# Routed experts of a two-layer hybrid block: the down product as one unsplit fp32 matmul a block

## The chip, the cores and the metric

The kernel runs on one core of one Trainium2 chip. The metric is the device time of one execution in microseconds (us); smaller is better. Three runs of the kernel before took 1002.78, 1001.38 and 1005.39 us, median 1002.78.

## The reference, cut to what matters

The model is a chain of a Mamba-1 mixer, a mixture-of-experts layer, a Mamba-2 mixer with a gated MLP, and the same mixture-of-experts layer again, over 2048 tokens of width 128. The change touches only the two mixture-of-experts layers, and of these only the routed experts:

```
x         = tokens, 2048 x 128
prob      = softmax(x @ gate_weight.T)          # 8 experts
top 2 experts of each token, weights normalised
routed(x) = sum over the two experts e of weight * swiglu(x, gate_up[e], down[e])
swiglu(x, gate_up, down):
    h = x @ gate_up.T                           # 128 -> 2 * 938
    g, u = split(h)
    return (silu(g) * u) @ down.T               # 938 -> 128
```

The output adds a shared expert of the same shape, which every token passes, and the residual.

## The kernel before, in words

`ffn_stage` is built twice, with the tags `f` (first layer) and `g` (second); `f_` and `g_` begin the tiles' names in the profile. Tokens are sorted by expert into 39 tiles (`SLOT_TILES`) of 128 token slots. Each expert's slots are padded to whole tiles. A table, filled at run time, tells for each tile its expert and where the expert's weights lie: a ring of three places (`RING`), each holding an expert's gate-up weights (2 x 938 columns) and down weights (8 blocks, `TILES`, of 128 rows, the last with 42 real ones).

Most products of the layer are made in split precision. A number is cut into a high part, rounded to fp32r (the format that TensorE takes in one reduced-precision product), and a low part, which is the rest. Three products of parts (high by high, high by low, low by high) make one accurate product. `raw_ring` and `ring` are the same memory under two types: plain fp32, and rounded fp32r. SyncE loads an expert's raw weights into `raw_ring` (`load_expert`), and GpSimd splits them in four parts in `split_part`: part 0 copies the gate-up weights to their high half (L1047), part 1 the down weights (L1049), part 2 writes the low half of gate-up (L1052), part 3 that of down (L1055) and raises `w_ready`. Which part follows which gather of token rows or which store of result rows on GpSimd's queue is written out by hand (`BEHIND_GATHER`, `BEHIND_STORE`). Expert n+3 is loaded once the last product with expert n is summed.

TensorE's order for tile j (L1247 on) is: transpose the 128 token rows of tile j (`turn_row`, L1229); down product of tile j-2 (`down_tile`, L1214 and L1217); transpose the products silu(g) * u of tile j-1 (`turn_products`, L1196, eight blocks); gate and up products of tile j in two halves of columns (`expert_half`, L1243 to L1245, twelve matmuls). Token tiles and products stand in pairs of buffers by the tile's parity.

In `down_tile` each of the eight blocks takes two matmuls. The first (L1214) has the high part of the turned products (`q_hi`) as its stationary operand, and 256 moving columns: the high and the low half of the down weights side by side. Its results lie in the columns 0 to 127 and 128 to 255 of the PSUM bank `Y2`. The second (L1217) has the low part `q_lo` stationary and the 128 high columns moving; the last block has none. Its 42 real rows have their low part in further rows of the same stationary tile, from row 64 (`UT`) on, against a second copy of the weights there. So there are 15 matmuls a tile. After them ScalarE scales the cross columns by the tokens' share into `cross` (`crossed`, L1400), VectorE adds them to the main columns times the share and writes the result rows (`finish`, L1752), and GpSimd stores the rows (L1078).

The turned products are 1024 columns in two PSUM banks. ScalarE copies both halves to `q_hi` (L1395), VectorE subtracts that from PSUM and writes `q_lo` (L1742), and for the last block's tail one more small subtraction into `q_hi` (L1746). ScalarE's SiLU is L1418, VectorE's product L1773. TensorE waits for these through `q_low`, and before it writes the bank of the next down product, for `outs_ready`.

Of the kernel before, what the change touches and what calls it, by code (L numbers as in the profile page):

```python
# [16 lines left out]
P = 128  # L17
BATCH, SEQ = 2, 1024
T = BATCH * SEQ
CH = 512  # L20
# [23 lines left out]
EW = 2 * GW + 2 * TILES * P  # L44
# [794 lines left out]
def ffn_stage(k, d, which, tag, cleared, ready, out=None, logs=None, following=None):  # L839
# [39 lines left out]
    cross = work[:, 2 * H0:2 * H0 + 2 * P].rearrange("p (b m) -> p b m", b=2)  # L879
# [13 lines left out]
    def gathered(j):  # L893
# [9 lines left out]
        prods_ready, prods_turned, q_high, q_low, cross_ready, outs_ready, both_ready, tokens_ready, out_added, \  # L903
# [5 lines left out]
            "prods_ready prods_turned q_high q_low cross_ready outs_ready both_ready tokens_ready out_added "  # L909
# [14 lines left out]
    LAST_ROWS = UT + 2  # L924
# [51 lines left out]
    def down_of(ring, place):  # L976
        return ring[:, place, 2 * GW:EW].rearrange("p (i h m) -> p i h m", i=TILES, h=2)

    with stage, nc.Block(no_gpsimd_drain=True) as block:  # L979

        @block.sync
        def _(sp):
            def load_expert(n):
                place = (n - 1) % RING
                low, dn, done = raw_ring[:, place, GW:2 * GW], down_of(raw_ring, place), w_loaded[place]
                sp.dma_start(low[:, 0:INTER], d["gu"][n - 1, :, 0:INTER]).then_inc(done, 16)
                sp.dma_start(low[:, INTER:GW], d["gu"][n - 1, :, INTER:GW]).then_inc(done, 16)
                sp.dma_start(dn[:, :, 1, :], d["dn"][n, :, :].rearrange("(i p) m -> p i m", p=P)).then_inc(done, 16)
# [44 lines left out]
        def _(pool):  # L1033
            PARTS, STORES = 4, 2
            GROUPS = [0] + list(range(4, SLOT_TILES, 2))
            BEHIND_GATHER = {3: [(2, 0), (2, 1), (2, 2), (2, 3)], 5: [(3, 0)], 7: [(3, 1)], 9: [(3, 2)], 11: [(3, 3)],
                             17: [(4, 0)], 19: [(4, 1)], 21: [(4, 2)], 23: [(4, 3)],
                             33: [(5, 0), (5, 1), (5, 2), (5, 3)], 35: [(6, 0), (6, 1)], 37: [(6, 2)], 38: [(6, 3)]}
            BEHIND_STORE = {1: [(7, 0)], 3: [(7, 1), (7, 2), (7, 3)], 7: [(8, 0)], 9: [(8, 1)], 11: [(8, 2)], 13: [(8, 3)]}

            def split_part(n, part):
                place = (n - 1) % RING
                high, low, dn = ring[:, place, 0:GW], ring[:, place, GW:2 * GW], down_of(ring, place)
                raw, raw_dn = raw_ring[:, place, GW:2 * GW], down_of(raw_ring, place)
# [53 lines left out]
        def _(pe):  # L1098
# [31 lines left out]
            def gate_up(q):  # L1130
# [15 lines left out]
                if q == NPRE + 2:  # L1146
                    pe.wait_ge(q_low, 2 * SLOT_TILES)
# [58 lines left out]

            def down_tile(j):
# [141 lines left out]
        def _(act):  # L1349
# [57 lines left out]
            def tile(j):  # L1407
                if j:
                    turned(j)
                if j >= 2:  # L1410
                    crossed(j - 2)
# [53 lines left out]
            crossed(SLOT_TILES - 2)  # L1465
            evac(SLOT_TILES - 1)
            silu(NPRE)
            crossed(SLOT_TILES - 1)
# [35 lines left out]
        def _(dve):  # L1504
# [232 lines left out]
            def evac(j):  # L1737
                for half in range(2):
                    dve.wait_ge(q_high, 2 * j + half + 1)
                    n = CH - half * P  # L1740
                    a = slice(half * CH, half * CH + n)
                    last = nc.vector.tensor_tensor(q_lo[:, j % 2, a], ps[:, TR + half, 0:n],  # L1742
                                                   q_hi[:, j % 2, a].bitcast(F32), ALU.subtract)
                    if half:
# [1007 lines left out]
```

## Time and profile before

| What | Value |
|---|---|
| median of 3 runs | 1002.78 us |
| the profiled execution's own time | 1002.86 us |
| its span | 1001.0 us |
| TensorE matmul busy | 953.4 us (95%), 4711 records |
| TensorE weight load busy | 676.2 us (68%) |
| VectorE busy | 725.1 us (72%) |
| ScalarE busy | 569.8 us (57%) |
| GpSimd busy | 616.6 us (62%) |
| DMA | 69.71 MB, 70 GB/s on the mean |

In the rows, PE is TensorE's matmul, PEld its weight load, which overlaps matmuls, PEldq the sequencer that feeds them, DVE VectorE, ACT ScalarE, POOL GpSimd. A record's duration runs from its start to its modelled end, so durations of pipelined matmuls overlap; what one costs in a dense stream is the distance from its start to the start of the next. A plain fp32 matmul shows as two records of PE and two of PEld, a transpose or an fp32r matmul as one of each.

### The profile page before, as it was taken

To read this page: it belongs to the slowest core of one execution; us is meant where nothing else is said; L and a number is where in the kernel's file an instruction comes from. 1 tells how busy PE (TensorE), PEld (TensorE's weight loads), DVE (VectorE), ACT (ScalarE), POOL (GpSimd) and SP (SyncE) were. 2 spreads that over 40 slices of the span, in tenths; PEclk is the share of its full clock that TensorE was granted. 3 is DMA by queue.
4 is the path that set the end of the run, shared out by engine and by line. 5 is a ranking of instruction groups with operands and counts; after the bars stand their busy time and mean duration, and the time that the engine had idled before them with its cause. 6 is when DMAs were issued, how large, how long until landed. Compare 5 with 4: busy or idle time off the path is not lost. (4 is left out here: it accounts for less than half of the span.)

```text
span 1001.0 us, 16162 instructions
## 1 busy us (share of the span) xinstructions
PE 953.4 (95%) x4711; PEld 676.2 (68%) x4711; DVE 725.1 (72%) x1192; ACT 569.8 (57%) x1046; POOL 616.6 (62%) x482
## 2 busy tenths in 40 slices
PE   7988999988999999999999999998999999999997
PEld 2323333332467799899998556666666999999996
DVE  3999998999588666566665797775597666566666
ACT  6764655655542555555554788787723555555553
POOL 1599897999531856686541397852305764967432
PEclk9999989998999999999999999999999999999999
DMA  5233223353341123232011300000702222421104
GB/s 158 67 77 80 77 82 71 90 118 86 112 123 55 33 84 89 75 82 81 28 33 42 112 1 1 2 1 1 225 0 71 79 68 64 123 74 31 33 24 132
DMA packets 69248, 69.71 MB, mean 70 GB/s; under 512 B 14952, under 2 KB 51568, under 8 KB 69168
## 3 DMA queue, kind: packets, MB, share of 16 engines
q1 hardware_dynamic: 64176, 58.44, 20.2%
q0 software_dynamic: 4992, 10.23, 3.7%
q8 instruction: 46, 0.75, 0.3%
q14 instruction: 34, 0.28, 0.1%
HBM read 58.00 MB, written 10.62 MB: 69 GB/s over the span
## 5 line engine op out<-in xcount | busy, mean ns | idle before, releaser
L810 POOL TENSOR_TENSOR a_hc<-a_h,a_c_sb 128x512 f32<-128x512 f32 x128 | 159.7, 1272 | 45.1 <-DVE a_h L711 45.0
L492 PE MATMUL ps<-a_hc,eye 128*128 128x512 f32 x256 | 134.5, 641 | 12.6 <-POOL a_hc L810 12.0
L629 ACT ACTIVATE ps<-a_delta,a_neg_a 128x512 f32<-128x512 f32 x128 | 87.1, 689 | 73.5 <-DVE a_h L711 70.6
L492 PEld LDWEIGHTS ps<-a_hc,eye 128*128 128x128 f32 x256 | 45.6, 195 | 80.3 <-POOL a_hc L810 43.8
L1067 POOL DMA_INDIRECT f_rows<-xn_rows,f_source x39 | 37.4, 958 | 70.1 <-DVE f_source L1700 35.5
L1067 POOL DMA_INDIRECT g_rows<-xn_rows,g_source x39 | 37.3, 956 | 69.1 <-DVE g_source L1700 38.1
L711 DVE TENSOR_TENSOR_SCAN a_h<-ps,a_state,a_b_u 128x512 f32<-128x512 f32 x64 | 79.0, 1278 | 1.0 <-ACT ps L629 0.8
L1214 PE MATMUL ps<-g_ring_rounded,g_q_hi_rounded 128*128 x312 | 77.1, 337 | 0.0
L1214 PE MATMUL ps<-f_ring_rounded,f_q_hi_rounded 128*128 x312 | 77.0, 337 | 0.0
L711 DVE TENSOR_TENSOR_SCAN a_h<-ps,a_b_u 128x512 f32<-128x512 f32 x64 | 75.2, 1212 | 1.9 <-ACT ps L629 1.7
L691 DVE TENSOR_TENSOR a_b_u<-a_du,ps 128x1024 f32<-128x1024 f32 x57 | 68.5, 1202 | 0.9 <-PE ps L479 0.8
L1078 POOL DMA_INDIRECT token_rows<-f_rows,f_back x39 | 38.0, 975 | 49.0 <-DMA token_rows<-f_rows,f_back 23.3
L1078 POOL DMA_INDIRECT token_rows<-g_rows,g_back x39 | 38.0, 975 | 44.2 <-DMA token_rows<-g_rows,g_back 19.2
L1243 PE MATMUL ps<-f_ring_rounded,f_work_rounded 128*128 x156 | 62.1, 398 | 3.0 <-POOL f_ring_rounded L1055 1.8
L1773 DVE TENSOR_TENSOR f_prods<-f_work,ps 128x470 f32<-128x470 f32 x78 | 50.3, 644 | 18.0 <-PE ps L1245 14.3
L1243 PE MATMUL ps<-g_ring_rounded,g_work_rounded 128*128 x156 | 62.0, 397 | 1.0 <-DVE g_work_rounded L1758 0.6
L1418 ACT ACTIVATE f_work<-ps 128x470 f32<-128x470 f32 x78 | 44.0, 565 | 32.8 <-PE ps L1245 30.7
L1418 ACT ACTIVATE g_work<-ps 128x470 f32<-128x470 f32 x78 | 44.0, 564 | 30.2 <-PE ps L1245 27.4
L1773 DVE TENSOR_TENSOR g_prods<-g_work,ps 128x470 f32<-128x470 f32 x78 | 50.3, 644 | 14.9 <-PE ps L1245 11.1
L1217 PE MATMUL ps<-f_ring_rounded,f_q_lo_rounded 128*128 x273 | 60.9, 223 | 0.0
L1217 PE MATMUL ps<-g_ring_rounded,g_q_lo_rounded 128*128 x273 | 60.9, 223 | 0.0
L1214 PEld LDWEIGHTS ps<-g_ring_rounded,g_q_hi_rounded 128*128 128x128 f32 x312 | 58.9, 189 | 2.8
(485 smaller groups left out, 2753.3 us busy)
## 6 DMA issues: line engine op xcount, KB each, us to landing
a_c_sb<-c_rows SPq DMA_DIRECT2D x64, 256.0 KB, 3.3
f_ring<-in_gu SPq DMA_DIRECT2D x16, 469.0 KB
g_ring<-in_gu SPq DMA_DIRECT2D x16, 469.0 KB
f_ring<-in_dn SPq DMA_DIRECT2D x8, 512.0 KB
g_ring<-in_dn SPq DMA_DIRECT2D x8, 512.0 KB
xn_rows<-f_work SPq DMA_DIRECT2D x8, 256.0 KB, 4.1
f_rows<-token_rows SPq DMA_DIRECT2D x8, 256.0 KB, 4.7
xn_rows<-g_work SPq DMA_DIRECT2D x8, 256.0 KB, 4.1
```

The lines of the kernel that those rows point to most:

```text
L492: nc.tensor.matmul(ps[:, Y + f, :], k.eye[:, :], hc[:, s % WAITING, :], start=False, stop=(n == NST - 1)).then_inc(y_added, 1)
L629: nc.scalar.activation(ps[:, A + m % NA, :], delta[:, f, cols(g)], ACT.Exp, scale=neg_a[:, f, n:n + 1])\
L691: nc.vector.tensor_tensor(decayed_in[:, p:p + FT, :], du[:, :, cols(g)], ps[:, B + i % 2, :].unsqueeze(1).to_broadcast([P, FT, CH]), ALU.m ...
L711: nc.vector.tensor_tensor_scan(h[:, s % DEPTH, :], ps[:, A + m % NA, :], decayed_in[:, m % FEED, :], initial, ALU.mult, ALU.add).then_inc( ...
L810: nc.gpsimd.tensor_tensor(hc[:, m % WAITING, :], h[:, s % DEPTH, :], c_sb[:, i % RING, :], ALU.mult)\
L1067: nc.gpsimd.indirect_dma_start(rows[:, j, :], None, k.xn_rows, bass.IndirectOffsetOnAxis(ap=source[:, j:j + 1], axis=0))\
L1078: nc.gpsimd.indirect_dma_start(k.token_rows, bass.IndirectOffsetOnAxis(ap=back[:, j:j + 1], axis=0), rows[:, j, :], None).then_inc(sent, 16)
L1214: last = nc.tensor.matmul(ps[:, Y2, 0:2 * P], q_hi[:, j % 2, a], in_ring(place, w, w + 2 * P), start=(i == 0), stop=(i == NI), skip_group_ ...
L1217: nc.tensor.matmul(ps[:, Y2, 0:P], q_lo[:, j % 2, a], in_ring(place, w, w + P), start=False, stop=False, skip_group_check=True)
L1243: nc.tensor.matmul(out, xt[:, 0, j % 2, :], w_hi, start=True, stop=False)
L1418: nc.scalar.activation(gates[:, half, 0:HALVES[half]], ps[:, 2 * half, 0:HALVES[half]], ACT.Silu)\
L1773: nc.vector.tensor_tensor(prods[:, j % 2, half * H0:half * H0 + HALVES[half]], gates[:, half, 0:HALVES[half]], ps[:, 2 * half + 1, 0:HALVE ...
```

## The change

The down product of the routed experts is made in plain fp32. The turned products go unsplit into `q_plain`, an fp32 view of the memory that `q_hi` is in; the first half is copied by ScalarE, the second by VectorE. The down weights stay as SyncE loads them, in `raw_ring`, now packed as 8 x 128 columns; GpSimd splits only gate and up. Each block is one matmul of 128 moving columns, the last with 42 contraction rows. ScalarE alone scales the result by the share and writes the rows. The hand-written lists of GpSimd have two parts an expert in place of four.

```diff
-EW = 2 * GW + 2 * TILES * P
+DN = 2 * GW
+EW = DN + TILES * P + 376
...
-            PARTS, STORES = 4, 2
+            PARTS, STORES = 2, 2
             GROUPS = [0] + list(range(4, SLOT_TILES, 2))
-            BEHIND_GATHER = {3: [(2, 0), (2, 1), (2, 2), (2, 3)], 5: [(3, 0)], 7: [(3, 1)], 9: [(3, 2)], 11: [(3, 3)],
-                             17: [(4, 0)], 19: [(4, 1)], 21: [(4, 2)], 23: [(4, 3)],
-                             33: [(5, 0), (5, 1), (5, 2), (5, 3)], 35: [(6, 0), (6, 1)], 37: [(6, 2)], 38: [(6, 3)]}
-            BEHIND_STORE = {1: [(7, 0)], 3: [(7, 1), (7, 2), (7, 3)], 7: [(8, 0)], 9: [(8, 1)], 11: [(8, 2)], 13: [(8, 3)]}
+            BEHIND_GATHER = {3: [(2, 0), (2, 1)], 5: [(3, 0)], 9: [(3, 1)], 17: [(4, 0)], 21: [(4, 1)],
+                             33: [(5, 0), (5, 1)], 35: [(6, 0)], 37: [(6, 1)]}
+            BEHIND_STORE = {1: [(7, 0)], 3: [(7, 1)], 7: [(8, 0)], 9: [(8, 1)]}
...
                 if part == 1:
-                    nc.gpsimd.tensor_copy(dn[:, :, 0, :], raw_dn[:, :, 1, :]).then_inc(w_high, 1)
-                if part == 2:
-                    pool.wait_ge(w_high, 2 * n - 1)
-                    nc.gpsimd.tensor_tensor(low, raw, high.bitcast(F32), ALU.subtract)
-                if part == 3:
-                    pool.wait_ge(w_high, 2 * n)
-                    nc.gpsimd.tensor_tensor(dn[:, :, 1, :], raw_dn[:, :, 1, :], dn[:, :, 0, :].bitcast(F32),
-                                            ALU.subtract).then_inc(w_ready, 1)
+                    pool.wait_ge(w_high, n)
+                    nc.gpsimd.tensor_tensor(low, raw, high.bitcast(F32), ALU.subtract).then_inc(w_ready, 1)
...
             def turn_products(j):
                 pe.wait_ge(prods_ready, 2 * j + 2)
                 if j:
-                    pe.wait_ge(q_low, 2 * j)
+                    pe.wait_ge(q_first, j)
+                    pe.wait_ge(q_last, j)
                 for i in range(TILES):
-                    m = LAST_ROWS if i == NI and j else P
+                    m = TAIL if i == NI and j else P
...
             def down_tile(j):
                 place = ring_place(j)
-                pe.wait_ge(q_low, 2 * j + 2)
+                pe.wait_ge(q_first, j + 1)
                 if j:
                     pe.wait_ge(outs_ready, j)
                 for i in range(TILES):
-                    a, w = slice(i * P, (i + 1) * P), 2 * GW + 2 * i * P
-                    last = nc.tensor.matmul(ps[:, Y2, 0:2 * P], q_hi[:, j % 2, a], in_ring(place, w, w + 2 * P),
-                                            start=(i == 0), stop=(i == NI), skip_group_check=True)
-                    if i < NI:
-                        nc.tensor.matmul(ps[:, Y2, 0:P], q_lo[:, j % 2, a], in_ring(place, w, w + P),
-                                         start=False, stop=False, skip_group_check=True)
+                    if i == TILES // 2:
+                        pe.wait_ge(q_last, j + 1)
+                    last = nc.tensor.matmul(ps[:, Y2, 0:P], q_plain[0:k_of(i), j % 2, i * P:(i + 1) * P],
+                                            down_weights(place, i), start=(i == 0), stop=(i == NI))
                 last.then_inc(summed, 1)
...
             def evac(j):
-                for half in range(2):
-                    act.wait_ge(prods_turned, 2 * j + half + 1)
-                    nc.scalar.activation(q_hi[:, j % 2, half * CH:(half + 1) * CH], ps[:, TR + half, :], ACT.Copy)\
-                        .then_inc(q_high, 1)
-
-            def crossed(j):
+                act.wait_ge(prods_turned, 2 * j + 1)
+                if j >= 2:
+                    act.wait_ge(summed, NPRE + j - 1)
+                nc.scalar.activation(q_plain[:, j % 2, 0:CH], ps[:, TR, :], ACT.Copy).then_inc(q_first, 1)
+
+            def finish(j):
                 act.wait_ge(summed, NPRE + j + 1)
-                nc.scalar.activation(cross[:, j % 2, :], ps[:, Y2, P:2 * P], ACT.Copy, scale=share[:, j:j + 1])\
-                    .then_inc(cross_ready, 1)
+                nc.scalar.activation(rows[:, j, :], ps[:, Y2, 0:P], ACT.Copy, scale=share[:, j:j + 1])\
+                    .then_inc(outs_ready, 1)
...
             def evac(j):
-                for half in range(2):
-                    dve.wait_ge(q_high, 2 * j + half + 1)
...
-            def finish(j):
...
+                dve.wait_ge(prods_turned, 2 * j + 2)
+                if j >= 2:
+                    dve.wait_ge(summed, NPRE + j - 1)
+                nc.vector.tensor_copy(q_plain[:, j % 2, CH:], ps[:, TR + 1, :]).then_inc(q_last, 1)
```

## Rows read from the trace of the kernel before

**Rows 1.** The page's first part: engines over the span.

```profile
PE 953.4 (95%) x4711; PEld 676.2 (68%) x4711; DVE 725.1 (72%) x1192; ACT 569.8 (57%) x1046; POOL 616.6 (62%) x482
```

**Rows 2.** Windows: busy us (records) of each engine, PEclk; both expert stages.

```profile
326.00:545.00 219.00, 215.23 (x1439) 198.28 (x1437) 133.27 (x282) 115.48 (x243) 136.08 (x102) 1.00 0.20 58
...
765.00:980.00 215.00, 213.31 (x1432) 197.51 (x1431) 132.43 (x280) 114.10 (x239) 135.81 (x101) 1.00 0.20 59
```

**Rows 3.** Groups of PE by line: shapes xcount | busy us, mean ns | idle.

```profile
L1214 PE MATMUL ps<-f_ring_rounded,f_q_hi_rounded 128*128 x312 | 77.0, 337 | 0.0
...
L2110 PE MATMUL ps<-b_y,b_w_out 128*128 128x512 f32 x16 | 7.5, 592 | 0.0
```

**Rows 4.** Timeline of one steady tile: start us, us, engine, line.

```profile
520.48 0.19 PEld L1214 LDWEIGHTS ps<-f_ring_rounded,f_q_hi_rounded 128*128 128x128 f32 x1
...
520.59 0.19 PEld L1217 LDWEIGHTS ps<-f_ring_rounded,f_q_lo_rounded 128*128 128x128 f32 x1
...
520.71 0.19 PEld L1214 LDWEIGHTS ps<-f_ring_rounded,f_q_hi_rounded 128*128 128x128 f32 x1
...
522.24 0.86 PEld L1196 LDWEIGHTS ps<-eye,f_prods 128*128 128x128 f32 x8
...
523.10 0.19 PEld L1243 LDWEIGHTS ps<-f_ring_rounded,f_work_rounded 128*128 128x128 f32 x1
...
525.75 0.19 PEld L1214 LDWEIGHTS ps<-f_ring_rounded,f_q_hi_rounded 128*128 128x128 f32 x1
```

**Rows 5.** Weight loads of unsplit fp32 products, 128 moving columns.

```profile
289.70 0.30 PEld L1178 LDWEIGHTS ps<-f_chosen,masks 128*128 128x128 f32 x2 [1.51 <-DVE f_chosen L1566]
289.91 0.30 PEld L1179 LDWEIGHTS ps<-f_chosen,one 128*128 128x128 f32 x2
290.14 0.19 PEld L1126 LDWEIGHTS ps<-f_x_hi,sh_gu_rounded 128*128 128x128 f32 x1
```

**Rows 6.** Weight loads of fp32 products, 4 moving columns.

```profile
577.33 3.54 PEld L2024 LDWEIGHTS ps<-b_w_in,b_xp 128*128 128x128 f32 x31 [0.24 <-issue]
580.79 0.30 PEld L2000 LDWEIGHTS ps<-b_xp,b_w_in 128*128 128x128 f32 x2
```

**Rows 7.** Timeline of PE: fp32 products, 512 moving columns.

```profile
661.45 1.88 PE L2110 MATMUL ps<-b_y,b_w_out 128*128 128x512 f32 x4
```

**Rows 8.** PE's sequencer (PEldq) at L1214 and L1232, same tile.

```profile
L1214 PEldq FUSED_REGOPS  x8: 46/46/60, 519.8 to 520.8; - x8
...
L1232 PEldq TENSOR_LOAD <-f_table x1: 308/308/308, 521.5 to 521.5; - x1
```

**Rows 9.** Timeline of POOL, then of PE: split of the fifth expert.

```profile
413.25 1.78 POOL L1047 CAST f_ring_rounded<-f_ring 128x1876 fp32r<-128x1876 f32 x1
414.94 1.06 POOL L1049 CAST f_ring_rounded<-f_ring 128x1024 fp32r<-128x1024 f32 x1
415.94 4.24 POOL L1052 TENSOR_TENSOR f_ring_rounded<-f_ring,f_ring_rounded 128x1876 fp32r<-128x1876 f32 x1
420.12 2.36 POOL L1055 TENSOR_TENSOR f_ring_rounded<-f_ring,f_ring_rounded 128x1024 fp32r<-128x1024 f32 x1
...
419.80 1.03 PE L1196 MATMUL ps<-eye,f_prods 128*128 128x128 f32 x8
422.63 0.47 PE L1243 MATMUL ps<-f_ring_rounded,f_work_rounded 128*128 x1 [1.80 <-POOL f_ring_rounded L1055]
```

**Rows 10.** Groups of DVE and ACT in the first expert stage.

```profile
L1742 DVE TENSOR_TENSOR f_q_lo_rounded<-ps,f_q_hi_rounded 128x512 fp32r<-128x512 f32 x39 | 27.0, 692 | 13.1 <-ACT f_q_hi_rounded L1395 12.2 <-issue 0.9
...
L1752 DVE SCALAR_TENSOR_TENSOR f_rows<-ps,f_share,f_work 128x128 f32<-128x128 f32 x39 | 13.7, 351 | 53.1 <-ACT f_work L1400 51.8 <-issue 1.3
...
L1395 ACT ACTIVATE f_q_hi_rounded<-ps 128x512 fp32r<-128x512 f32 x78 | 42.4, 596 | 3.6 <-PE ps L1196 1.1
```

**Rows 11.** Windows of one tile: POOL busy throughout, POOL idle.

```profile
854.59:859.86 5.27, 5.27 (x37) 4.93 (x36) 3.28 (x7) 2.84 (x7) 5.27 (x2) 1.00 0.01 3
...
896.75:902.02 5.27, 5.27 (x38) 4.91 (x37) 3.27 (x7) 2.83 (x7) 0.00 (x0) 1.00 0.91 294
```

More of the change, by code:

```diff
@@ L902, in ffn_stage @@
         low_ready, summed, x_added, rest_zero, x_turned, xt_high, xt_low, gates_ready, ups_ready, gates_silu, \
-        prods_ready, prods_turned, q_high, q_low, cross_ready, outs_ready, both_ready, tokens_ready, out_added, \
+        prods_ready, prods_turned, q_first, q_last, outs_ready, both_ready, tokens_ready, out_added, \
         stored = sems(
@@ L908, in ffn_stage @@
             "low_ready summed x_added rest_zero x_turned xt_high xt_low gates_ready ups_ready gates_silu "
-            "prods_ready prods_turned q_high q_low cross_ready outs_ready both_ready tokens_ready out_added "
+            "prods_ready prods_turned q_first q_last outs_ready both_ready tokens_ready out_added "
             "stored")
@@ L974, in wide @@
         return v[:, :].unsqueeze(2).to_broadcast([P, TT, EXPERTS])
-    def down_of(ring, place):
-        return ring[:, place, 2 * GW:EW].rearrange("p (i h m) -> p i h m", i=TILES, h=2)
+    q_plain = norm_sq
     with stage, nc.Block(no_gpsimd_drain=True) as block:
@@ L984, in load_expert @@
                 place = (n - 1) % RING
-                low, dn, done = raw_ring[:, place, GW:2 * GW], down_of(raw_ring, place), w_loaded[place]
+                low, done = raw_ring[:, place, GW:2 * GW], w_loaded[place]
+                dn = raw_ring[:, place, DN:DN + TILES * P].rearrange("p (i m) -> p i m", i=TILES)
                 sp.dma_start(low[:, 0:INTER], d["gu"][n - 1, :, 0:INTER]).then_inc(done, 16)
                 sp.dma_start(low[:, INTER:GW], d["gu"][n - 1, :, INTER:GW]).then_inc(done, 16)
-                sp.dma_start(dn[:, :, 1, :], d["dn"][n, :, :].rearrange("(i p) m -> p i m", p=P)).then_inc(done, 16)
+                sp.dma_start(dn[:, :, :], d["dn"][n, :, :].rearrange("(i p) m -> p i m", p=P)).then_inc(done, 16)
             sp.dma_start(plain_dn[:, :, :], d["dn"][0, :, :].rearrange("(i p) m -> p i m", p=P)).then_inc(plain_loaded, 16)
@@ L1146, in gate_up @@
                 if q == NPRE + 2:
-                    pe.wait_ge(q_low, 2 * SLOT_TILES)
+                    pe.wait_ge(q_last, SLOT_TILES)
                 if i < NI:
@@ L1205, in in_ring, with down_weights @@
                 return ring[:, bass.ds(place, 1), a:b].rearrange("p r m -> p (r m)")
+            def down_weights(place, i):
+                a = DN + i * P
+                return raw_ring[0:k_of(i), bass.ds(place, 1), a:a + P].rearrange("p r m -> p (r m)")
             def down_tile(j):
                 place = ring_place(j)
-                pe.wait_ge(q_low, 2 * j + 2)
+                pe.wait_ge(q_first, j + 1)
                 if j:
@@ L1410, in tile @@
                 if j >= 2:
-                    crossed(j - 2)
+                    finish(j - 2)
                 if j >= 1:
@@ L1464, in _ @@
                 tile(j)
-            crossed(SLOT_TILES - 2)
+            finish(SLOT_TILES - 2)
             evac(SLOT_TILES - 1)
             silu(NPRE)
-            crossed(SLOT_TILES - 1)
+            finish(SLOT_TILES - 1)
             for q in range(NPRE + 1, NQ):
@@ L1737, in evac @@
             def evac(j):
-                for half in range(2):
-                    dve.wait_ge(q_high, 2 * j + half + 1)
[L1740 to L1744, printed above, removed]
-                        a = slice(NI * P, TILES * P)
-                        last = nc.vector.tensor_tensor(q_hi[UT:UT + TAIL, j % 2, a], ps[0:TAIL, TR + 1, n:CH],
-                                                       q_hi[0:TAIL, j % 2, a].bitcast(F32), ALU.subtract)
-                    last.then_inc(q_low, 1)
-            def finish(j):
-                dve.wait_ge(cross_ready, j + 1)
-                nc.vector.scalar_tensor_tensor(out=rows[:, j, :], in0=ps[:, Y2, 0:P], scalar=share[:, j:j + 1],
-                                               in1=cross[:, j % 2, :], op0=ALU.mult, op1=ALU.add)\
-                    .then_inc(outs_ready, 1)
+                dve.wait_ge(prods_turned, 2 * j + 2)
+                if j >= 2:
+                    dve.wait_ge(summed, NPRE + j - 1)
+                nc.vector.tensor_copy(q_plain[:, j % 2, CH:], ps[:, TR + 1, :]).then_inc(q_last, 1)
             def turned(j):
@@ L2724, in layout @@
     m["dn"][:, :INTER] = np.concatenate([a("L0_ffn_shared_down")[None], a("L0_ffn_experts_down")]).transpose(0, 2, 1)
-    m["dn"][1:, full + UT:full + UT + TAIL] = m["dn"][1:, full:INTER]
     m["w_gateF"] = a("L0_ffn_gate_weight").T
```

9 lines of the change are left out of this document (1 added, 8 removed).

## The prediction

> **What bounds the kernel now.** I read the engines' busy times, then windows by stage, then the groups of TensorE, then the timeline of single tiles, and at last the places where TensorE stood still. TensorE is busy for 953.4 of 1001.0 us [rows 1]. That alone says little, since records overlap. In the two stages of the routed experts, the only ones that the change touches, PE is busy for 215.23 of 219 and 213.31 of 215 us at a granted clock of 1.00, the 2.4 GHz level, while DVE has 133.27 and 132.43 us of work, ACT 115.48 and 114.10, POOL 136.08 and 135.81 [rows 2]. A steady tile takes 5.27 us, from the first weight load of one down product at 520.48 to that of the next at 525.75 [rows 4], and so it is in a window where POOL is busy throughout and in one where POOL does nothing [rows 11]. So TensorE alone sets the pace of 78 tiles (39 in each layer), and I look for what the change does to its stream.
>
> The down block runs from its first weight load at 520.48 to the first of the transposes at 522.24: 1.76 us for 15 matmuls, 0.117 us each. The transposes take 0.86 us, up to 523.10, gate and up 2.65 us, up to 525.75 [rows 4]. What bounds the down block? Its PE records last 337 ns for 256 moving columns [rows 3], but that is a latency. A steady stream of other products tells: 31 weight loads of 128 columns, with only 4 moving columns behind each, take 3.46 us (577.33 to 580.79), 0.1116 us each [rows 6]. A down matmul costs hardly more than its weight load. Its block is a chain of weight loads, and the number of columns that each moves is nearly free.
>
> **The change part by part.**
>
> *The matmuls.* Out go 8 of 256 columns and 7 of 128, with 15 weight loads. In come 8 plain fp32 matmuls. The trace shows each such as two records with two weight loads (the four loads below come from two matmuls), so 16 loads replace 15. The number of instructions in the source halves, that of the weight loads doesn't. What one record costs in such a stream the trace shows in short pieces. Two unsplit fp32 products with 128 moving columns load at 289.70 (twice), 289.91 (twice), and the next product at 290.14: 0.44 us for four, 0.110 each [rows 5]. A stream of fp32 records with 512 columns shows 4 in 1.88 us; one record lasts 0.592 us, so the distance is (1.88 - 0.592) / 3 = 0.43 us, a quarter of it 0.1075 for 128 columns [rows 3, 7]. So streaming and loading are about equal here, and I take 0.111, between the 0.110 of the same shape and the 0.1116 of pure loading. The block then costs 16 x 0.111 = 1.776 us against 1.76: +0.016 a tile, 78 x 0.016 = +1.2 us. The bounds: from below the pure stream, 16 x 0.1075 = 1.72, -0.04 a tile, -3.1 us. From above the dearest interval of the present block, in which a weight load lies beside a stream of 256 columns: 520.59 to 520.71, 0.12 us [rows 4]. 16 x 0.12 = 1.92, +0.16 a tile, +12.5 us.
>
> Here the Trainium skill speaks against the change: by FP8 and Floating Point Precision, section TensorE Precision Notes, a true fp32 product is four passes through the array. By columns alone the new block would be 8 x 4 x 128 = 4096 against 8 x 256 + 7 x 128 = 2944, 1.39 times the old, which on 1.76 us would be +0.69 us a tile, +54 us. The records agree that there is more than one pass (two records a product), but the old block isn't bound by columns: 2944 of them in a stream of 0.43 / 1024 us each would be 1.24 us, not 1.76 [rows 4, 7]. So I don't take this sum.
>
> *TensorE's sequencer.* The eight operations that put the run-time address in take 46 ns each and lie between 519.8 and 520.8, so they are done 1.4 us before the block ends at 522.24; the table load for the gate-up products comes at 521.5 [rows 4, 8]. Even if each of the 16 records wanted such an operation (8 x 46 ns = 0.37 us more), 520.8 would become 521.2, still before 521.5. I cost it at nothing; without this cover it would be 0.37 us a tile, 29 us. The new waits in the block (`q_first` at its start, `q_last` at its fifth block) are for copies that begin right after the transposes of the tile before, at 523.10, 2.65 us ahead of the block at 525.75. Behind the waiting matmul stand the rest of the block, the transposes and gate-up, so a late copy would stop everything; but the copies are short.
>
> *ScalarE and VectorE.* ScalarE had two copies of 596 ns a tile, now one; VectorE had a subtraction of 692 ns over 512 columns, a second one over 384, and one over the tail, now one copy of 512, at most as dear as the 692 [rows 10]. The final step was one instruction on each engine, VectorE's of 351 ns [rows 10]; now ScalarE's alone, which frees PSUM for the next block 0.35 us earlier. In a tile of 5.27 us ScalarE is busy for 2.84 and VectorE for 3.28 [rows 11]; with 0.60 and more than 0.8 us less they wait more. TensorE gains nothing by that, since PE had no idle time in such a window. On ScalarE the final step stands ahead of the copy and the two SiLUs, as before. 0 us.
>
> *GpSimd.* Per expert 1.06 us (copy) and 2.36 us (subtraction) go, 3.4 us of 9.4. Nearly all of it was hidden; one place was not. In layer f the fifth expert's split ran from 413.25 to 422.48 and TensorE, done with its transposes, waited for its last part and began at 422.63 [rows 9]. From the pattern of a tile the gate-up product follows 0.79 us after the first transpose matmul (a record of the transposes begins at 419.80; the loads of 0.86 us in rows 4 say the same less one overlap), so it was due at 420.6: a loss of 2.03 us. Now the split is 1.78 + 4.24 less small overlaps, 413.25 to 419.3 even if it starts no sooner, 1.3 us before 420.6. What is late next is nothing: TensorE runs on. -2.0 us. In g such a wait doesn't occur: PE is busy for the whole tile in which POOL is busiest [rows 11]. With less split work the gathers and stores come earlier too; their queue is not waited for by TensorE in steady tiles.
>
> *The rest.* The loads by SyncE keep their size and count; only their place in memory is packed. The last transpose takes 42 rows for 66, in a stream bound by its moving side: 0. The last tile's rows are stored 0.35 us sooner, but the shared expert's products fill TensorE after it: 0.
>
> **The sum** is made against the profiled execution's own 1002.86 us (span 1001.0 and 1.86 around it), which is 0.08 us over the median of the runs shown: 1002.86 + 1.2 - 2.0 = 1002.1 us.
>
> **The rivals.**
>
> *Load and stream don't overlap fully (slower).* Place: the interval between two records of the new block. In the present block an interval in which a load lies beside 256 columns costs 0.12 against 0.11 where it lies beside 128 [rows 4]; an fp32 record of 128 columns may keep the array as long as 256. If all 16 cost 0.12, the time is 1002.86 + 12.5 - 2.0 = 1013.3 us; it decides from 0.111 on, and at 0.1125 it has eaten the gain on GpSimd (16 x 0.0015 x 78 = 1.9 us). For it: the rows of the present block. Against it: the four loads at 0.110, which are of exactly this type and width, though only four. Its middle, 0.116, gives 1002.86 + 0.096 x 78 - 2.0 = 1008.4 us.
>
> *The stream sets the pace at its best rate (faster).* 0.1075 a record, 1.72 us a block: 1002.86 - 3.1 - 2.0 = 997.7 us. For it: 0.1075 from the 512-column stream and 0.86 / 8 = 0.1075 of the transposes [rows 4, 7]. Against it: the pure load at 0.1116 [rows 6], which every fp32 record has as well.
>
> *Relief of the other engines speeds the remaining stream (faster).* Twelve gate-up matmuls take 2.65 us [rows 4]. If they were held up by other engines' traffic, a few per cent could come back: 2% of it is 0.05 us a tile, 4 us, which gives 998. Against it: the tile is 5.27 us with POOL at full load and at none [rows 11].
>
> *The split isn't hidden (the change doesn't do all it says).* The new order on GpSimd's queue could move the fifth expert's split behind a gather that lands later, and the 2.0 us stay: 1004.1 us. Against it: the same gather (33) comes first and 10 us of earlier splits (three experts, 3.4 us each) are gone from the queue.
>
> **How the numbers follow.** The likeliest case, with its neighbour in which the split is not hidden, has 0.58 (range 999.5 to 1005.5). The two faster rivals together have 0.20, the slower one 0.22. This kernel's runs tell no change from one within about 0.5%, 5 us: below 997.8 is faster, above 1007.8 slower. Of the faster rivals about three quarters of the chance lies below 997.8, and a little comes from sources that I don't see, so 0.18; of the slower one most lies above 1007.8, 0.20; the rest, 0.62, within. The range that leaves out 2 in 10 reaches from 997 to 1010 us. The forecast is 1002 us.
>
> **What would show it.** In the trace after, the down block should be 16 weight loads in a row at 0.11 us, from the first to the transposes 1.77 us, and a tile 5.28 us. At 1.9 us the first rival is right, at 1.72 the second. Gate and up should still take 2.65 us; less would be the third. The wait for GpSimd near 420 us should be gone, else the fourth. If the tile lasts longer with gaps on PE, a new wait or the sequencer has come on the path, and the prediction is wrong in a step that I cost at nothing. It would also be wrong if an fp32 record with a run-time address costs far from 0.11 us; no row shows that pair of properties together.

## The result, and the profile after

The changed kernel takes 1030.4 us (median of 4 runs), the one before 1003.2 us beside it: a ratio of 1.0269, with a 95% interval of 1.0234 to 1.0305. It is 27 us slower. The forecast was 1002 us, no change.

The page's first part of the kernel after (its span is 1029.9 us) shows the same share of TensorE, 78 of its records more (one a tile, 16 in place of 15), and less work on the three other engines:

```profile
PE 982.2 (95%) x4789; PEld 686.5 (67%) x4789; DVE 639.3 (62%) x958; ACT 532.0 (52%) x968; POOL 560.2 (54%) x450
```

The windows of the two expert stages, with the columns of [rows 2]:

```profile
326.00:545.00 219.00, 217.05 (x1398) 192.79 (x1397) 87.33 (x161) 91.78 (x193) 110.63 (x86) 1.00 0.19 59
...
765.00:980.00 215.00, 213.19 (x1354) 187.56 (x1354) 90.41 (x170) 88.05 (x184) 109.73 (x85) 1.00 0.22 64
```

PE is as full as before, while DVE falls from about 133 to 87 and 90 us and POOL from 136 to 110. A small part of that fall comes from the tiles being longer, so that fewer fit into the same window: in the kernel with full rows below, whose tiles are about as long as before, the same windows have 92 and 90 us of DVE and 114 and 112 of POOL. The work taken from these two engines is gone, and it bought nothing. One steady tile tells where the time went; this is its timeline, as in [rows 4]:

```profile
504.11 2.06 PEld L1211 LDWEIGHTS ps<-f_ring,f_q_hi 128*128 128x128 f32 x16
...
506.29 0.82 PEld L1188 LDWEIGHTS ps<-eye,f_prods 128*128 128x128 f32 x8
...
507.11 0.19 PEld L1237 LDWEIGHTS ps<-f_ring_rounded,f_work_rounded 128*128 128x128 f32 x1
...
509.78 2.06 PEld L1211 LDWEIGHTS ps<-f_ring,f_q_hi 128*128 128x128 f32 x16
```

A tile lasts 5.67 us (504.11 to 509.78), not 5.27. The down block lasts 2.18 us to the first transpose at 506.29, where it was 1.76. The transposes take 0.82 us, where they had 0.86, and gate and up 2.67, where they had 2.65. So the loss is in the down block. In narrow windows of the same tile one sees single weight loads. First three in the middle of the down block:

```profile
505.23 0.41 PEld L1211 LDWEIGHTS ps<-f_ring,f_q_hi 128*128 128x128 f32 x3
```

Three loads of 0.19 us end 0.41 us after the first began, so (0.41 - 0.19) / 2 = 0.11 us lie between them. And the block's last two loads, of 42 rows:

```profile
505.87 0.29 PEld L1211 LDWEIGHTS ps<-f_ring,f_q_hi 42*128 42x128 f32 x2
```

They too are 0.11 us apart. The last load of 128 rows before them, and the second of the two alone:

```profile
505.56 0.19 PEld L1211 LDWEIGHTS ps<-f_ring,f_q_hi 128*128 128x128 f32 x1
...
505.98 0.19 PEld L1211 LDWEIGHTS ps<-f_ring,f_q_hi 42*128 42x128 f32 x1
```

So the first load of 42 rows, at 505.87, comes 0.31 us after the load before it. The next load of 128 rows, the transposes', comes at 506.29, again 0.31 us after the one at 505.98. Twice a tile, an interval is 0.2 us longer than elsewhere. The groups of weight loads of the first layer say the same. The loads themselves are not longer with 42 rows (184 ns in the mean, against 192). The idle time before them (the last figure) is 4.7 us, which over 39 tiles is 0.12 us each: 0.31 less the 0.19 that the load before took.

```profile
L1211 PEld LDWEIGHTS ps<-f_ring,f_q_hi 128*128 128x128 f32 x546 | 64.1, 192 | 2.8
...
L1211 PEld LDWEIGHTS ps<-f_ring,f_q_hi 42*128 42x128 f32 x78 | 11.5, 184 | 4.7
```

### The profile page after: what moved, and what is told of

It is laid out like the page before. It is cut to its first block and busy times, and to the rows that moved or that the text cites. A ratio compares the mean times of both kernels' runs of the same rounds, so it can differ in the third digit from the quotient of the medians.

```text
span 1029.9 us, 16121 instructions
## 1 busy us (share of the span) xinstructions
PE 982.2 (95%) x4789; PEld 686.5 (67%) x4789; DVE 639.3 (62%) x958; ACT 532.0 (52%) x968; POOL 560.2 (54%) x450
## 5 line engine op out<-in xcount | busy, mean ns | idle before, releaser
L811 POOL TENSOR_TENSOR a_hc<-a_h,a_c_sb 128x512 f32<-128x512 f32 x128 | 159.5, 1269 | 44.8 <-DVE a_h L712 44.7
L493 PE MATMUL ps<-a_hc,eye 128*128 128x512 f32 x256 | 133.3, 633 | 15.3 <-POOL a_hc L811 14.5
L493 PEld LDWEIGHTS ps<-a_hc,eye 128*128 128x128 f32 x256 | 44.6, 193 | 82.9 <-POOL a_hc L811 47.5
L1211 PE MATMUL ps<-f_ring,f_q_hi 128*128 (+1 forms) x624 | 83.5, 281 | 0.0
L1211 PE MATMUL ps<-g_ring,g_q_hi 128*128 (+1 forms) x624 | 83.5, 281 | 0.0
L1211 PEld LDWEIGHTS ps<-f_ring,f_q_hi 128*128 128x128 f32 (+1 forms) x624 | 75.6, 191 | 7.5
L1211 PEld LDWEIGHTS ps<-g_ring,g_q_hi 128*128 128x128 f32 (+1 forms) x624 | 75.6, 191 | 7.5
L1735 DVE COPY f_q_hi<-ps 128x512 f32<-128x512 f32 x39 | 27.0, 692 | 84.7 <-PE ps L1188 84.7
L1735 DVE COPY g_q_hi<-ps 128x512 f32<-128x512 f32 x39 | 27.0, 691 | 84.3 <-PE ps L1188 84.3
L692 DVE TENSOR_TENSOR a_b_u<-a_du,ps 128x1024 f32<-128x1024 f32 x57 | 68.0, 1193 | 0.1
```

Source lines behind the costliest of these rows:

```text
L493: nc.tensor.matmul(ps[:, Y + f, :], k.eye[:, :], hc[:, s % WAITING, :], start=False, stop=(n == NST - 1)).then_inc(y_added, 1)
L692: nc.vector.tensor_tensor(decayed_in[:, p:p + FT, :], du[:, :, cols(g)], ps[:, B + i % 2, :].unsqueeze(1).to_broadcast([P, FT, CH]), ALU.m ...
L811: nc.gpsimd.tensor_tensor(hc[:, m % WAITING, :], h[:, s % DEPTH, :], c_sb[:, i % RING, :], ALU.mult)\
L1211: last = nc.tensor.matmul(ps[:, Y2, 0:P], q_plain[0:k_of(i), j % 2, i * P:(i + 1) * P], down_weights(place, i), start=(i == 0), stop=(i == ...
L1735: nc.vector.tensor_copy(q_plain[:, j % 2, CH:], ps[:, TR + 1, :]).then_inc(q_last, 1)
```

## The experiments

**All rows in the last block.** One size was changed in the changed kernel. The rows from 43 on carry zero weights, so that the sum is the same.

```diff
+            def down_rows(i):
+                return P
...
-                return raw_ring[0:k_of(i), bass.ds(place, 1), a:a + P].rearrange("p r m -> p (r m)")
+                return raw_ring[0:down_rows(i), bass.ds(place, 1), a:a + P].rearrange("p r m -> p (r m)")
...
-                    last = nc.tensor.matmul(ps[:, Y2, 0:P], q_plain[0:k_of(i), j % 2, i * P:(i + 1) * P],
+                    last = nc.tensor.matmul(ps[:, Y2, 0:P], q_plain[0:down_rows(i), j % 2, i * P:(i + 1) * P],
```

> The changed kernel, but the last block's down matmul takes all 128 contraction rows, of which 86 carry zero weights, in place of 42. Theory (a change of the number of rows between two matmuls stops TensorE from loading the next weights early): in the changed kernel the weight load of the 42-row record starts 0.312 us after the load before it and the next 128-row load 0.306 us after the last of 42 rows, against 0.112 elsewhere in the block. With 128 rows throughout all 16 intervals are 0.11 us, the down block takes 1.79 us, a tile 5.28, and the time falls by 78 x 0.395 = 31 us from 1030.4 to about 999 to 1002 us. Rival 1 (these records are slow because they are the last ones of the accumulation, or because they wait for something at the boundary to the transposes): nothing changes, 1030 us. Rival 2 (unsplit fp32 with a run-time address is slow as a whole): at most a few us less than 1030.

Measured: 1005.2 us against 1002.6 of the kernel before beside it, ratio 1.0015 (0.9989 to 1.0041). The loss is gone. The timeline of weight loads in a tile:

```profile
511.68 1.87 PEld L1214 LDWEIGHTS ps<-f_ring,f_q_hi 128*128 128x128 f32 x16
513.47 0.87 PEld L1188 LDWEIGHTS ps<-eye,f_prods 128*128 128x128 f32 x8
514.34 0.19 PEld L1240 LDWEIGHTS ps<-f_ring_rounded,f_work_rounded 128*128 128x128 f32 x1
...
517.01 1.08 PEld L1214 LDWEIGHTS ps<-f_ring,f_q_hi 128*128 128x128 f32 x9
```

Sixteen loads in 1.79 us (511.68 to 513.47), 0.112 each, the last interval like the others. The tile is 5.33 us (511.68 to 517.01). This settles where the loss comes from: the 42 rows of the last block.

**How many rows, and where the border is.** The same edit with 96, 97, 65 and 64 rows in the last block, one kernel each.

```diff
+            def down_rows(i):
+                return P if i < NI else 65          # 96, 97, 65, 64
```

> The changed kernel with 96 contraction rows in the last block (54 of them with zero weights). Theory in its form 'any other number of rows': 1030 us as with 42, intervals 0.31 us on both sides of the block's last two records. In its form 'the array is cut into four groups of 32 rows and a different number of groups counts': also 1030, since 96 rows are three groups. Rival (few rows are slow in themselves): less than 1030, near 1010.

> The changed kernel with 97 contraction rows in the last block (55 of them with zero weights). Any other number of rows counts: 1030 us, intervals 0.31 us. Only the number of 32-row groups counts (97 rows touch all four): all intervals 0.11 us, about 1001 us as with 128 rows.

> The changed kernel with 65 contraction rows in the last block (23 of them with zero weights). 96 and 97 rows cost nothing and 42 rows 0.4 us a tile; in the first mixer 64 rows pay too (0.948 us from a 128-row load to a 64-row one, 0.429 usual). If the border lies between 64 and 65 rows (half the array), 65 rows cost nothing: about 1005 us, intervals of 0.11. If it lies elsewhere between 65 and 96, 1030 us and intervals of 0.31.

> The changed kernel with 64 contraction rows in the last block (22 of them with zero weights). With 65 rows all intervals were 0.112 us and the time 1006 us. If the border is half the array: intervals of 0.31 us on both sides, as with 42 rows, and 1030 us. If it lies lower (the mixer's 64-row loads being late for another reason): 1006 us.

Measured: 96 rows 1006.0 us (ratio 1.0031), 97 rows 1004.7 us (1.0017), 65 rows 1006.2 us (1.0016), 64 rows 1033.6 us (1.0302, 1.0284 to 1.032). That any change of the number of rows counts, as I first thought, is wrong, and so is that the number of 32-row groups counts: 96 rows, three groups, gave both away. In the traces with 96 and with 97 rows, too, the down block takes 1.78 to 1.79 us. The two kernels at the border, first 64 rows, then 65:

```profile
500.57 2.06 PEld L1214 LDWEIGHTS ps<-f_ring,f_q_hi 128*128 128x128 f32 x16
502.74 0.82 PEld L1188 LDWEIGHTS ps<-eye,f_prods 128*128 128x128 f32 x8
```

```profile
500.19 1.86 PEld L1214 LDWEIGHTS ps<-f_ring,f_q_hi 128*128 128x128 f32 x16
501.97 0.87 PEld L1188 LDWEIGHTS ps<-eye,f_prods 128*128 128x128 f32 x8
```

Sixteen loads and the step to the transposes take 2.17 us with 64 rows (500.57 to 502.74) and 1.78 with 65 (500.19 to 501.97). So what costs is the step between more than 64 rows and 64 or fewer; 65, 96 and 97 rows are all free.

**The step or the small number.** In two kernels more blocks have 42 rows. Products are left out in both.

```diff
# e4: blocks 3 and 7          # e5: blocks 4 to 7
+ return TAIL if i in (3, NI) else P
+ return TAIL if i >= 4 else P
```

> The changed kernel with 42 contraction rows in the fourth block as well as in the last, so that the number of rows changes four times a tile in place of two; this leaves 86 of the fourth block's products out of the sum. Theory (a change between 128 rows and 64 or fewer costs about 0.2 us, at each change): two more changes, 78 x 0.395 = +31 us over the changed kernel, 1061 us, a tile of 6.06 us. Rival (the cost belongs to the end of the block): 1030 us.

> The changed kernel with 42 contraction rows in the last four blocks in place of the last one; this leaves products of three blocks out of the sum. The number of rows still changes twice a tile. Theory (the change costs, not the small number of rows): 1030 us, intervals of 0.11 us among the eight 42-row records. Rival (each short load is slow, or short matmuls are cheaper): 78 x 3 x 0.4 = +94 us, or less than 1030.

Measured: e4 1065.4 us (ratio 1.0601), e5 1030.1 us (1.0251). Two short blocks apart cost about twice as much as one; four in a row cost as much as one. The timelines of e4 and of e5:

```profile
504.00 2.44 PEld L1214 LDWEIGHTS ps<-f_ring,f_q_hi 128*128 128x128 f32 x16
506.56 0.82 PEld L1188 LDWEIGHTS ps<-eye,f_prods 128*128 128x128 f32 x8
```

```profile
500.18 2.05 PEld L1214 LDWEIGHTS ps<-f_ring,f_q_hi 128*128 128x128 f32 x16
502.35 0.82 PEld L1188 LDWEIGHTS ps<-eye,f_prods 128*128 128x128 f32 x8
...
505.83 2.05 PEld L1214 LDWEIGHTS ps<-f_ring,f_q_hi 128*128 128x128 f32 x16
```

In e4 the down block takes 2.56 us (504.00 to 506.56 in its trace), 0.38 more than in the changed kernel, for two more steps; the first two had cost 0.39 (2.18 against 1.79). In e5, 2.17 us with eight short records. A step costs 0.2 us in either direction, short records cost nothing.

**The kernel before with a short last matmul.** Is it unsplit fp32 that makes it so? Here the last split-precision matmul takes 42 rows; this leaves out the low part of the tail's products.

```diff
-                    last = nc.tensor.matmul(ps[:, Y2, 0:2 * P], q_hi[:, j % 2, a], in_ring(place, w, w + 2 * P),
+                    m = P if i < NI else TAIL
+                    last = nc.tensor.matmul(ps[:, Y2, 0:2 * P], q_hi[0:m, j % 2, a], in_ring(place, w, w + 2 * P, m),
...
```

> The kernel before, but the last split-precision down matmul of each tile (256 moving columns) takes 42 contraction rows in place of 128; this leaves out the low part of the tail's products. Theory: the step belongs to the number of rows and not to unsplit fp32, so it comes here too: one 42-row load, late on its own side behind a 128-column stream of 0.053 us (0.25 us after the load before it in place of 0.12) and the next 128-row load late behind a 256-column stream (0.31 in place of 0.14), +0.30 us a tile, 78 x 0.30 = +23 us, about 1026 us. Rival (only unsplit fp32 records with few rows are slow): 1003 us, no change.

Measured: 1025.1 us, ratio 1.0221 (1.0171 to 1.0271), as the theory said. The weight loads at the end of its down block:

```profile
503.77 0.19 PEld L1215 LDWEIGHTS ps<-f_ring_rounded,f_q_hi_rounded 128*128 128x128 f32 x1
503.88 0.19 PEld L1218 LDWEIGHTS ps<-f_ring_rounded,f_q_lo_rounded 128*128 128x128 f32 x1
504.15 0.18 PEld L1215 LDWEIGHTS ps<-f_ring_rounded,f_q_hi_rounded 42*128 42x128 f32 x1
504.46 0.83 PEld L1196 LDWEIGHTS ps<-eye,f_prods 128*128 128x128 f32 x8
```

The load of 42 rows comes 0.27 us after the one before, where [rows 4] has 0.12, and the transposes' comes 0.31 us after that. In the kernel before, the last load stands 0.14 us ahead of the transposes' at 522.24:

```profile
522.10 0.19 PEld L1214 LDWEIGHTS ps<-f_ring_rounded,f_q_hi_rounded 128*128 128x128 f32 x1
```

The first of the two steps is cheaper; the matmul that is waited for there moves 128 columns of fp32r, that of the second 256. So the step doesn't belong to unsplit fp32. The kernel before has none, because its last matmul takes all 128 rows, the low part of the tail among them.

**The same step in the first mixer.** The matmul at L480 takes 64 rows between others of 128. On top of e1:

```diff
-    sel = sb("sel", [64, NST, P], F32R)
-    rows = sb("rows", [64, T], F32R)
+    sel = sb("sel", [P, NST, P], F32R)
+    rows = sb("rows", [P, T], F32R)
...
+            nc.gpsimd.memset(sel[64:P, :, :].bitcast(F32), 0.0).then_inc(sel_set, 1)
+            nc.gpsimd.memset(rows[64:P, :].bitcast(F32), 0.0).then_inc(sel_set, 1)
```

> The kernel of e1_full_rows, and in the first mixer the matmul that spreads the rows of B over the partitions takes 128 contraction rows (64 of them zero on both sides) in place of 64. Theory: there too the weight load is again made early. 53 times the interval into it falls from 0.948 to 0.429 us and 43 times the one out of it from 0.43 to about 0.23: 27 + 9 = 36 us less TensorE time in a stage of 266 us. But VectorE is busy for 235 of these 266 us, so most of it should be idle time of TensorE: 0 to -8 us, I take 1002 us. Rival (TensorE paces the mixer): 36 us off, 970 us. Rival (the 64 rows were never the cause there): the intervals stay.

Measured: 1000.1 us, ratio 0.9963 (0.9939 to 0.9987). The weight loads around the 64-row one in the changed kernel:

```profile
149.77 0.19 PEld L493 LDWEIGHTS ps<-a_hc,eye 128*128 128x128 f32 x1 [0.24 <-issue]
150.20 0.19 PEld L493 LDWEIGHTS ps<-a_hc,eye 128*128 128x128 f32 x1 [0.24 <-issue]
151.15 0.18 PEld L480 LDWEIGHTS ps<-a_rows,a_sel 64*128 64x128 f32 x1 [0.76 <-DVE a_b_u L692]
151.57 0.30 PEld L493 LDWEIGHTS ps<-a_hc,eye 128*128 128x128 f32 x2 [0.24 <-issue]
```

With 128 rows in that matmul:

```profile
150.02 0.19 PEld L493 LDWEIGHTS ps<-a_hc,eye 128*128 128x128 f32 x1 [0.24 <-issue]
150.45 0.19 PEld L480 LDWEIGHTS ps<-a_rows,a_sel 128*128 128x128 f32 x1 [0.24 <-issue]
150.88 0.42 PEld L395 LDWEIGHTS ps<-a_xp,a_w_tap 128*128 128x128 f32 x2 [0.24 <-issue]
```

The interval into it falls from 0.95 us (150.20 to 151.15) to 0.43 (150.02 to 150.45). The profile had put the idle time before that load down to VectorE (L692); with 128 rows that wait is not there at this place, so it was the step.

These 0.52 us are not what the step costs, though. Even where the load is made early, its matmul has to wait until the one before has streamed, and one sees that in the interval after next. Over three intervals, from the load before L480 to the second load behind it, the changed kernel takes 1.48 us (150.20 to 151.68, since the last two loads are 0.30 - 0.19 = 0.11 apart) and the kernel with 128 rows 1.09 (150.02 to 151.11, since its last two are 0.42 - 0.19 = 0.23 apart). So entering and leaving cost 0.39 us together, 0.2 a step, as in the down block. There are 57 such loads, and 57 x 0.39 would be 22 us (the 36 us of the expectation counted the entry at 0.52), but the time falls by 5. The groups of weight loads of the first 266 us tell where the rest went, first with 64 rows (e1), then with 128; the figure behind the second bar is the idle time before them:

```profile
L493 PEld LDWEIGHTS ps<-a_hc,eye 128*128 128x128 f32 x256 | 45.2, 195 | 80.3 <-POOL a_hc L811 42.3 <-issue 37.8
...
L480 PEld LDWEIGHTS ps<-a_rows,a_sel 64*128 64x128 f32 x57 | 10.7, 189 | 46.9 <-issue 33.3 <-DVE a_b_u L692 12.9 <-ACT a_sz L620 0.8
```

```profile
L493 PEld LDWEIGHTS ps<-a_hc,eye 128*128 128x128 f32 x256 | 44.8, 194 | 99.0 <-POOL a_hc L813 65.6 <-issue 32.7
...
L480 PEld LDWEIGHTS ps<-a_rows,a_sel 128*128 128x128 f32 x57 | 11.5, 202 | 19.5 <-issue 14.0 <-DVE a_b_u L692 5.5
```

The idle time before L480 falls from 46.9 to 19.5 us, that before L493 rises from 80.3 to 99.0, in wait for GpSimd's products (L811, in e7 L813). VectorE, besides, is busy for 235 and 238 of the 266 us, as the windows show:

```profile
0.00:266.00 266.00, 241.14 (x485) 86.06 (x485) 235.15 (x228) 155.04 (x224) 215.54 (x170) 0.96 0.34 86
```

```profile
0.00:266.00 266.00, 231.32 (x505) 90.48 (x506) 237.57 (x229) 157.56 (x228) 219.00 (x172) 0.96 0.34 90
```

The intervals of the two ratios, of e1 and of e7, only just keep apart (0.9989 and 0.9987). The traces bear the gain out: from the first to the last matmul of L493 it is 218.3 us here and 218.9 in the last experiment below, which has the same edit, and 221.8 to 225.2 in the eleven traces with 64 rows.

The mixer's traces hold one more border. Behind the 64-row matmul there comes at some places one of 8 rows, in partitions 32 to 39 (from the changed kernel):

```profile
67.98 0.18 PEld L480 LDWEIGHTS ps<-a_rows,a_sel 64*128 64x128 f32 x1 [0.76 <-DVE a_b_u L692]
68.40 0.29 PEld L419 LDWEIGHTS ps<-a_x_rows,a_w_dt 8*128 8x128 f32 x2 [0.24 <-issue]
69.45 0.30 PEld L493 LDWEIGHTS ps<-a_hc,eye 128*128 128x128 f32 x2 [0.76 <-issue]
```

The first load of 8 rows comes 0.42 us after that of 64, as one of 128 rows does at 151.57, while two loads of 8 rows are 0.11 apart. So a step between 64 and 8 rows makes the load late as well, though both are at most 64. Whether that is by the number of rows or by their place, no run tested.

**The split of the fifth expert alone.** In the kernel before, one list entry is moved:

```diff
-                             33: [(5, 0), (5, 1), (5, 2), (5, 3)], ...
+                             31: [(5, 0), (5, 1), (5, 2), (5, 3)], ...
```

> The kernel before with one thing moved: the four parts of the fifth expert's split stand behind gather 31 in place of 33 on GpSimd's queue. In layer f that starts them at about 408.6 in place of 413.25 us, so that they end at 418 and not at 422.5, and TensorE needn't wait from 420.6 to 422.6. Theory: the one long tile of layer f (7.31 us) becomes 5.28, -2.0 us, 1001 us. Rival (the wait is taken over by a gather or another split): 1003 us, the long tile stays or another one is long.

Measured: 1000.4 us against 1003.5, ratio 0.9980 (0.9965 to 0.9996). The interval only just leaves out 1, but the trace shows the wait gone. The timeline of GpSimd's split, its first and its last part:

```profile
407.34 1.77 POOL L1047 CAST f_ring_rounded<-f_ring 128x1876 fp32r<-128x1876 f32 x1
...
414.20 2.41 POOL L1055 TENSOR_TENSOR f_ring_rounded<-f_ring,f_ring_rounded 128x1024 fp32r<-128x1024 f32 x1
```

It ends at 416.6, and TensorE goes from the transposes to gate and up without a wait, by PE's timeline:

```profile
418.38 1.03 PE L1196 MATMUL ps<-eye,f_prods 128*128 128x128 f32 x8
419.17 0.46 PE L1243 MATMUL ps<-f_ring_rounded,f_work_rounded 128*128 x1
```

The step is 0.79 us (418.38 to 419.17), where it was 2.83 [rows 9], and layer f's down blocks, from the start of the first to that of the last, take 200.6 us for 202.7.

**Both in the kernel before.** The early split and the mixer's 128 rows, with the split-precision down product of before.

> The kernel before with the early split of e6 and the 128-row spreading matmul of e7, and its own down product of 15 weight loads. Sum of what the parts gave: e7 took 5 us off e1 (1005.2 to 1000.1 us in their medians), the split should take 2.0, the down block of before is 0.05 us a tile shorter than e1's: 1002.8 - 5 - 2 = 996 us, faster than every kernel so far. Rival (the parts take the same time off): 998 to 1001 us.

Measured: 998.5 us, ratio 0.9951 (0.9939 to 0.9964). This is the fastest kernel of the study, 0.5% below the one before. Its own comparison doesn't show it to be faster than e7 (0.9963, 0.9939 to 0.9987), whose interval overlaps. The forecast of 996 was 2.5 us too good; the time lies where the rival had it, that the parts take the same time off. The trace doesn't bear the rival out, though. Both gains are in it: from the first to the last matmul of L492 it is 218.9 us, before 223.0, and layer f's down blocks take 200.7 us for 202.7. What is longer is the stretch from that last matmul to the first gate and up product of layer f, 71.3 us, where the twelve other traces have 67.9 to 70.2. Whether this kernel makes it longer or chance, one trace doesn't tell.

## Why the prediction was wrong

*The matmuls.* The step that failed is "The block then costs 16 x 0.111 = 1.776 us against 1.76". The price of a load was right: fourteen loads from 504.11 to 505.56 stand 0.11 us apart, and the kernel with full rows has all 16 in 1.79 us. What was wrong is that all sixteen had this price. I took the last block's two records, with 42 rows, for the same as the others, and the intervals into them and out of them are 0.31 us each in place of 0.11. The term was sized +0.016 us a tile, and the block measured +0.42; two steps of 0.2 are 0.40 of this. The transposes behind take 0.04 less, so the tile shown is 0.40 longer. 78 x 0.40 = 31 us less the 2.0 us on GpSimd is 29, and the spans differ by 28.9, the medians by 27. By layers, from the first down load to the last: g grew from 202.3 to 217.4 us (15.1), f, which had the wait of 2.0 to lose, from 204.4 to 217.2 (12.8). I had read 42 rows in the change and priced them for the transposes only, where 42 is a number of columns.

The trace of before held the evidence. In the first mixer it has the same late 64-row loads that the rows of the kernel after show above (0.95 us after the load before, at 49 of 57 places). I looked for rows of fp32 products with 128 columns, found four loads at 0.110 [rows 5], and called the case settled; all four had 128 rows. A matmul's shape has three sides, and I matched two.

*The mechanism, as far as the runs show it.* In a steady stream a weight load starts with the matmul before it. The timeline of PE has a matmul's record at 505.56, where the load for the next one begins:

```profile
505.56 0.69 PE L1211 MATMUL ps<-f_ring,f_q_hi 128*128 x3
```

Across the step the load starts later. The last matmul of 128 rows begins at 505.67 and the load of 42 rows at 505.87, 0.20 us on, which is the stream of its columns (0.107) and about 0.09 more. Its own matmul then waits for the load, another 0.11. So from matmul to matmul it takes the stream plus 0.2 us, where otherwise it takes the longer of stream and load. In the interval between loads this gives one sum: 0.11 (the load before) + the stream of the matmul before + about 0.09. With 128 columns of fp32 (0.107) that is 0.31, measured 0.31; with 128 columns of fp32r (0.053, an estimate as half of that) 0.26, measured 0.27. For the mixer's 512 columns of fp32, where the stream of one matmul more (0.43) stands in place of the load, 0.43 + 0.43 + 0.09 = 0.95, measured 0.95. Behind the mixer's 64-row matmul, 512 columns of fp32r (0.21, half of 0.43), it is 0.11 + 0.21 + 0.09 = 0.41, measured 0.42. The sum is fitted to these intervals and not tested by a run of its own, and that the load waits for the stream is read from this fit. Why the border lies at 64 rows stays open.

The Trainium skill says on its page TensorE: Matmul & The Clock Gate, section LDWEIGHTS (loading the stationary operand), that a weight load's time depends on its columns and not on its rows. The load itself agrees within 4%: 184 ns with 42 rows, 192 with 128. But what a load costs here is decided by when it may start, and that depends on the rows. The same page of the Trainium skill, section Part 3: Packing small matmuls — row/col tiling, says that weight loads overlap running matmuls only when they use other groups of rows, though its text also allows it for loads into a background buffer. The traces here don't bear out the "only": loads into all 128 rows started with matmuls on all 128 rows, and in e5 loads of 42 rows followed each other at 0.11 us too. Late were those across the border. Into which buffer a load goes, no trace here shows.

*The four passes.* The sum that I rejected (+54 us, by columns alone) was rightly rejected. With full rows the fp32 block costs 1.79 us against 1.76 of before, 0.112 and 0.117 a load, both close to the 0.1116 of [rows 6].

*The rival "load and stream don't overlap fully"* had the right side and the right block, not the mechanism. It spread 0.12 over all 16 records; in truth fourteen intervals are at 0.11 and two at 0.31. Its 1013.3 us was too low, and my range ended at 1010. The bound from above came from rows with 128 rows, and so it couldn't hold this.

*TensorE's sequencer.* Right, it is not on the path: the sequencer's operations for the block are still eight and are over before the first load at 504.11, as the line's source view shows (the numbers are the shortest, median and longest in ns, then the first and last start).

```profile
L1211 PEldq FUSED_REGOPS  x8: 46/46/60, 502.8 to 503.7; - x8
```

*ScalarE and VectorE.* Right: their work fell, and nothing came of it, since the tile is TensorE's.

*GpSimd.* Right in size, as e6 shows by itself: -3 us by the medians, -2.0 by the ratio, -2.0 in its trace (0.79 for 2.83). In the kernel after, the split and TensorE's step beside it are these:

```profile
415.09 1.76 POOL L1044 CAST f_ring_rounded<-f_ring 128x1876 fp32r<-128x1876 f32 x1
416.93 4.23 POOL L1047 TENSOR_TENSOR f_ring_rounded<-f_ring,f_ring_rounded 128x1876 fp32r<-128x1876 f32 x1
```

```profile
421.32 1.09 PE L1188 MATMUL ps<-eye,f_prods 128*128 128x128 f32 x8
422.17 0.46 PE L1237 MATMUL ps<-f_ring_rounded,f_work_rounded 128*128 x1
```

TensorE goes on after 0.85 us, not 2.83. I had the split start at 413.25, but it started at 415.09; TensorE had fallen behind by then, and the split, done at 421.16, was in time. With full rows TensorE is not behind, and there too the split (411.67 to 417.72) ends before TensorE needs it, and the step is 0.79 us.

*What remains of the forecast.* With the rows filled up, the kernel takes 1005.2 us where the forecast was 1002. Its tile is 5.33 us against 5.27 to 5.28, +0.05 where I had +0.016. The block gives 0.03 of it (1.79 against 1.76, where I had 1.776). In the two tiles shown the rest is in the transposes (0.87 us against 0.86) and in gate and up (2.67 against 2.65); over all tiles it is more in the transposes. Its cause I didn't test. That is 78 x 0.05 = 3.9 us less 2.0: +1.9 us, within the interval of its ratio of 1.0015. So the forecast would have fitted a kernel that this change didn't make.

## What to carry to other kernels

Keep the number of contraction rows over 64 through a stream of matmuls: zero rows that fill a short block up to 65 or more cost nothing, and a step across 64 costs about 0.2 us each way. Short matmuls in a row pay only where they begin and end, if they have the same rows (from 64 to 8 rows the load was late again). In a stage that TensorE doesn't pace, as the first mixer, most of the saving becomes idle time. When a new instruction is priced by a row of the old trace, match its contraction rows too, not only its type and its columns. And count weight loads, not matmuls: an unsplit fp32 product is two of them, so that halving the matmuls saved TensorE nothing.

## What the runs showed of the hardware that I had not expected

A step between more than 64 and at most 64 contraction rows delays the weight load until, by the fit above, the matmul before has streamed: intervals of 0.31 us in place of 0.11 with 128 moving columns of fp32, 0.27 with 128 of fp32r, 0.95 in place of 0.43 with 512 of fp32. On leaving it is late as well (0.31 in the down block). In time from matmul to matmul each step costs 0.2 us in the down block as in the mixer, where entering and leaving cost 0.39 together. It is the same for one short block as for four in a row (1030.4 and 1030.1 us). 65 rows are free (1006.2 us), 64 are not (1033.6 us). Between 64 and 8 rows the load was late too (0.42 us).
